# One decoder layer on one core: all five engines get another order of the same steps

## The reference

```python
x = x + attn(layernorm(x))        # attn(z) = z + out-projection; 16 heads of 8, softmax over 128 keys, biases
x = x + xattn(layernorm(x), ctx)  # 16 heads of 64, rope on q and k, key j seen by query i if i-32 <= j <= i
x = x + ffn(layernorm(x))
# ffn: e = argmax(x @ router.T) of 8 experts, for each token
#      y  = (silu(x @ gate[e].T) * (x @ up[e].T)) @ down[e].T      its own expert, hidden size 256
#      ys = the same with one shared expert;  result y + ys
```

## Time and profile before

| | |
|---|---|
| runs | 796.94, 797.93, 798.8 us; median 797.93 |
| profiled execution | 793.82 us, its span 791.7 us |
| TensorE | 755.8 us busy (95%), 11,796 MATMUL |
| TensorE weight loads | 610.1 us (77%) |
| VectorE, ScalarE, GpSimd | 541.6, 535.6, 526.1 us (68%, 68%, 66%) |
| mean granted clock of TensorE | 0.988 |

### The profile page before, as it was taken

One profiled execution on the slowest core, in us unless ns is written; L12 is line 12 of the kernel. 1 busy time (PEld: TensorE's weight loads), 2 busy tenths in 40 slices (PEclk: granted clock), 3 DMA queues, 4 the chain that ended last, 5 costly groups with the idle time before them and its releaser, 6 DMA issues.

```text
span 791.7 us, 31542 instructions
## 1 busy us (share of the span) xinstructions
PE 755.8 (95%) x11796; PEld 610.1 (77%) x11796; DVE 541.6 (68%) x1398; ACT 535.6 (68%) x1943; POOL 526.1 (66%) x857
## 2 busy tenths in 40 slices
PE   7999999999999999999999999999999999788995
PEld 5778888888888888888888888888888887666563
DVE  3467777777777777777777777777777778445663
ACT  2367777777777777777777777777777776664452
POOL 4466677666777677777767766677676776454454
PEclk8999999999999999999999999999999999999997
DMA  6000111001111000000000000000000000343340
GB/s 235 9 9 9 29 37 36 21 29 36 37 36 37 15 14 24 23 23 17 23 24 23 23 15 15 17 15 17 17 13 13 10 10 2 88 161 110 100 116 20
DMA packets 24563, 29.86 MB, mean 38 GB/s; under 512 B 3416, under 2 KB 20700, under 8 KB 24416
## 3 DMA queue, kind: packets, MB, share of 16 engines
q1 hardware_dynamic: 20912, 19.66, 8.2%
q0 software_dynamic: 2784, 6.56, 2.4%
q10 hardware_dynamic: 720, 1.63, 0.6%
HBM read 16.82 MB, written 11.47 MB: 36 GB/s over the span
## 4 chain that ended last, share of the span: by engine, by line
PE 91%; ACT 2%; issue 2%; DVE 2%; another core or an unknown queue 1%; DMA 1%; POOL 1%; POOLq 0%; SPq 0%; ACTq 0%; DVEq 0%
PE P L315 10%; PE P L280 8%; PE P L290 8%; PE P L356 7%; PE P L300 7%; PE P L342 5%; PE P L328 5%; PE P L232 4%; PE P L215 4%; PE P L247 4%; PE P L374 4%; PE P L421 4%; PE P L382 2%; PE P L255 2%; PE P L345 1%
## 5 line engine op out<-in xcount | busy, mean ns | idle before, releaser
L884 ACT ACTIVATE PX<-P,mx 128x128 f32<-128x128 f32 x512 | 182.4, 384 | 25.6 <-DVE mx L596 25.6
L596 DVE TENSOR_REDUCE mx<-P 128x4 f32<-128x512 f32 x128 | 81.2, 679 | 112.9 <-PE P L315 112.9
L1054 POOL TENSOR_TENSOR PX<-PX,mx 128x512 f32<-128x512 f32 x128 | 130.5, 1041 | 40.4 <-DVE mx L601 40.4
L884 ACT ACTIVATION_READ_ACCUMULATOR PX<-P,mx 128x1 f32 x512 | 114.6, 224 | 0.0
L893 ACT ACTIVATE PT<-P 128x512 f32<-128x512 f32 x128 | 69.9, 598 | 65.6 <-PE P L328 65.6
L848 ACT ACTIVATE PS<-P 128x512 f32<-128x512 f32 x128 | 66.1, 602 | 53.5 <-PE P L236 53.5
L1000 POOL TENSOR_SCALAR st<-st 128x1 f32<-128x1 f32 x96 | 22.1, 230 | 120.5 <-DVE st L504 116.8
L1049 POOL TENSOR_TENSOR rq<-rq,tq 128x1024 f32<-128x1024 f32 x32 | 75.6, 2364 | 24.8 <-DVE rq L560 24.8
L315 PE MATMUL P<-rk,rq 32*128 32x128 f32 x2048 | 85.1, 283 | 6.0 <-issue 5.7
L535 DVE TENSOR_REDUCE nmf<-P 128x4 f32<-128x512 f32 x128 | 79.5, 683 | 13.0 <-PE P L215 13.0
L315 PEld LDWEIGHTS P<-rk,rq 32*128 32x128 f32 x2048 | 71.4, 186 | 15.5 <-issue 14.8
(11 more groups left out here) (155 smaller groups left out, 1836.7 us busy)
## 6 DMA issues: line engine op xcount, KB each, us to landing
xrow<-z_xs SPq DMA_DIRECT2D x39, 136.0 KB
ew<-in_ew SPq DMA_DIRECT2D x9, 384.0 KB, 3.3
z_xs<-c SPq DMA_DIRECT2D x8, 408.0 KB
x<-in_x SPq DMA_DIRECT2D x32, 64.0 KB, 1.7
cxT<-in_ctxT SPq DMA_DIRECT2D x31, 64.0 KB, 1.7
z_xs<-c SPq DMA_DIRECT2D x8, 136.0 KB, 1.9
out<-yst,xrow POOLq DMA_INDIRECT x39
wk<-in_wk SPq DMA_DIRECT2D x1, 512.0 KB, 4.1
```

Of the source, the lines that this page charges most:

```text
L596: dve.tensor_reduce(mx[b % 3][:, 0, r, :], v3(bank(f"ds{r}")), AX.X, ALU.max, negate=True).then_inc(S["v_dm"][r], 1)
L884: t = act.activation(PX[(4 * b + r) % 6][:, c, :], p[:, c * 128:c * 128 + 128], ACT.Exp, bias=m[:, 0, r, c:c + 1], scale=1.0, accum_out=m[ ...
L1054: pool.tensor_tensor(X[:, :, :], X[:, :, :], mx[b % 3][:, 2, r, :].rearrange("p (h a) -> p h a", a=1).to_broadcast([128, 4, 128]), ALU.mul ...
```

## The change

No step's own code changes. What changes: the order of the steps in the loop body of all five engines, the banks of the steps (`BANK`), the filling products at the start (`WARM`, 182 before, 241 after), the number of periods (46 to 45), how many expert tiles lie in the loop (`LOOP`), and the order of the first loads. A helper `first` is added that nothing calls; without it `batch` does as before.

```diff
-LOOP = dict(xt=11, xg=10, xr=8, xy=8, xl=21)
+LOOP = dict(xt=13, xg=12, xr=10, xy=9, xl=21)
-WARM = {('a', 0): 36, ('a', 1): 14, ('nmt', 0): 43, ('kE', 1): 13, ('cnt', 0): 13, ('qO', 0): 9, ('ds0', 0): 22,
-        ('cnt', 1): 19, ('nmt', 2): 13}
-S0, PERIODS = 28, 46
+WARM = {('a', 0): 36, ('qkv', 0): 8, ('v1', 0): 17, ('s0', 0): 51, ('nmt', 0): 40, ('st0', 0): 9, ('oT', 0): 13,
+        ('ln', 0): 10, ('qO', 0): 8, ('ds0', 0): 10, ('oT', 1): 28, ('ln', 1): 11}
+S0, PERIODS = 28, 45
```

Going round it the form changes 11 times. GpSimd:

```diff
             for s in range(PERIODS):
-                batch(e_rstd, s - 6)
-                batch(b_rstd, s - 4)
                 batch(d_pn, s - 5, 3)
-                batch(d_pn, s - 5, 2)
+                tile(x_send, "xy", s - 36, 0)
+                batch(f_pos, s - 7)
+                batch(b_nm, s - 3)
...
+                batch(f_send, s - 7)
                 batch(r_ka, s - 3)
-                batch(b_nm, s - 3)
-                batch(f_pos, s - 7)
                 batch(r_qa, s - 4)
-                batch(f_send, s - 7)
+                batch(a_xab, s - 2)
...
                 batch(a_rstd, s)
                 batch(f_acc, s - 6)
-                batch(a_xab, s - 2)
+                batch(d_pn, s - 4, 0)
+                batch(e_rstd, s - 5)
                 batch(d_pn, s - 4, 1)
-                batch(d_pn, s - 4, 0)
+                batch(d_pn, s - 4, 2)
+                batch(b_rstd, s - 3)
```

More of the change, by code:

```diff
@@ L455, in _ @@
[L455 to L461, removed]
-                batch(d_s, s - 5)
+                tile(x_hT, "xr", s - 37, 2)
+                batch(b_x1, s - 5)
+                tile(x_up, "xg", s - 36, 0)
+                batch(b_s, s - 4)
+                tile(x_dn, "xy", s - 37, 2)
@@ new lines, in _ @@
+                batch(e_tr, s - 7)
+                tile(x_hT, "xr", s - 37, 3)
+                tile(x_tr, "xt", s - 36, 2)
+                batch(r_k, s - 4, 1)
+                batch(a_tr, s - 3)
+                tile(x_up, "xg", s - 36, 1)
+                batch(f_up, s - 7)
+                batch(b_ln, s - 5)
+                batch(d_t, s - 6, 0)
+                batch(d_t, s - 6, 1)
+                batch(r_q, s - 5, 1)
+                batch(b_nm, s - 4)
+                batch(r_q, s - 5, 0)
@@ new lines, in _ @@
+                tile(x_dn, "xy", s - 37, 3)
+                batch(d_pv, s - 6, 1)
+                batch(b_st, s - 4)
+                batch(d_pv, s - 6, 0)
+                batch(a_qkv, s - 3)
+                tile(x_hT, "xr", s - 36, 0)
+                tile(x_tr, "xt", s - 36, 3)
+                batch(c_v, s - 4, 0)
+                tile(x_up, "xg", s - 36, 2)
+                batch(d_s, s - 5)
+                tile(x_tr, "xt", s - 35, 0)
+                batch(b_pv, s - 4)
+                batch(d_wo, s - 6)
@@ L463, in _ @@
+                tile(x_dn, "xy", s - 36, 0)
+                tile(x_hT, "xr", s - 36, 1)
+                tile(x_up, "xg", s - 36, 3)
+                batch(f_pos, s - 7)
+                batch(b_oT, s - 4)
                 batch(r_k, s - 3, 0)
[L464 to L467, removed]
                 batch(f_dn, s - 7)
-                batch(a_qkv, s - 3)
-                batch(b_oT, s - 4)
@@ L471, in _ @@
-                batch(d_wo, s - 6)
+                tile(x_dn, "xy", s - 36, 1)
                 batch(b_cn, s - 4)
-                tile(x_up, "xg", s - 36, 1)
-                tile(x_dn, "xy", s - 37, 3)
-                batch(f_pos, s - 7)
[L476 to L482, removed]
@@ L751, in _ @@
             for s in range(PERIODS):
-                tile(x_gate, "xg", s - 37, 1)
-                batch(r_k3, s - 4)
-                tile(x_gate, "xg", s - 37, 2)
+                batch(d_max, s - 6, 1)
+                batch(d_max, s - 6, 3)
+                batch(d_ri, s - 6, 0)
+                batch(d_y, s - 7)
+                tile(x_y, "xy", s - 37, 0)
+                batch(b_cn, s - 5)
+                tile(x_gate, "xg", s - 37, 2)
+                batch(f_pos, s - 8)
+                batch(d_ri, s - 6, 1)
@@ L970, in _ @@
[L970 to L982, removed]
@@ L983, in _ @@
-                batch(b_oT, s - 4)
+                batch(f_th, s - 8)
+                batch(b_cT, s - 6)
+                batch(d_pt, s - 7, 0)
+                batch(d_pt, s - 7, 2)
+                batch(a_norm, s - 3)
+                batch(d_pt, s - 7, 3)
+                batch(d_pt, s - 7, 1)
+                batch(b_nmT, s - 5)
+                batch(d_ox, s - 7, 1)
+                batch(b_ps, s - 5, 1)
+                batch(d_ox, s - 7, 0)
+                tile(x_hT, "xr", s - 37, 0)
@@ new lines, in _ @@
+                tile(x_xT, "xt", s - 37, 3)
+                batch(b_ps, s - 5, 3)
+                batch(b_ps, s - 5, 2)
+                batch(b_ps, s - 5, 0)
+                batch(c_v, s - 5, 0)
+                tile(x_xT, "xt", s - 36, 0)
+                batch(a_q, s - 4)
+                tile(x_th, "xg", s - 37, 2)
+                batch(d_exp, s - 6, 0)
+                batch(b_oT, s - 5)
+                batch(d_exp, s - 6, 1)
+                tile(x_hT, "xr", s - 37, 1)
+                batch(d_exp, s - 6, 2)
```

129 lines of the change are left out of this document (53 added, 76 removed).

## The result

The kernel after takes 767.24 us (median of 4 runs, 765.12 to 768.98), the kernel before 797.43 beside it (4 runs, 796.87 to 798.8): ratio 0.9618, 95% interval 0.9589 to 0.9647. The forecast was 767. The profiled execution took 765.12 us, its span 763.0. Seven lines were added near the top of the file, so line 315 (`d_s`) is now 322, 261 (`b_cn`) is 268, 300 (`r_q`) is 307.

The account below looks back on a forecast made before the run. TensorE's own work bounds the kernel, so its start-to-start period sets the time. Span 791.7 - 24.6 + 2.8 - 6.2 - 1 - 2 = 760.7, plus 6.2 to the median gives 767 us; range 756 to 779.

Parts of the forecast that it names:

- the three middle terms: Middle periods: send moved -24.6 us, +2.8 for what may reach `d_pv`, two fewer tiling changes -6.2.
- Send: GpSimd's send moved from `d_s` to beside `r_q`: saves 0.91 us in each of 27 periods, -24.6 us.
- The +0.1 a period for `d_pv`: Allowance for the moved send's disturbance reaching the small products of `d_pv`: +2.8 us in all.
- Tilings: TensorE's tiling changes, 13 to 11 a period: 0.20 us a period, -6.2 us over 31 periods.
- Slacks: Waits between engines in the new order: all hidden by TensorE's work, costed at nothing; tightest slack 0.1 at `b_oT`.
- The GpSimd chain to `d_s`: Send, `r_ka`, then `r_qa`, which lets `d_s` start: done 11.1 us after `b_s`, slack 0.6.
- The slower rival: GpSimd chain to `d_s`: send and rotation adds 1.9 us longer, `d_s` waits 1.3 every period, 807 us; chance 0.07.
- Ends: Start, earlier loads against 59 more filling products: -1 us (-4 to +3); tail, earlier expert tiles: -2 (-6 to +3).
- From span to median: Added to the 760.7 us span: 2.1 around the span and 4.1 from execution to median, 6.2 in all.
- The stall goes with the send: Rival at the moved send: the 0.91 us a period is paid whatever runs beside it, 789 us; chance 0.10.
- new short waits: Rival at `b_oT` and `b_x1`: slack of 0.1 to 0.2 missing by 0.4 us a period, 779 us; chance 0.12.
- the order moves nothing: Rival: TensorE's work is the same and the pause only shifts to another step, same time; chance 0.03.

## Why the prediction was right

The time and the period were right, and the send's stall is shown; the split of the gain between the two parts was not. Spans of the two first traces, by `b_cn`: the forecast was -31.0, the trace has -28.7: -29.7 from the first to the 31st, where the three middle terms add up to -28.0, and +1.0 outside it, where the ends were forecast at -3.

- **Send** (forecast -24.6 + 2.8). The mechanism held in this: the pause was the send's, and large products cover it. Its fixed rate of 23 instructions a us didn't (77 beside a send in the new order), so why large products cover it stays open. The send came 5.57 after `b_s` (396.24 - 390.67; forecast 5.3). Its worth is 21.16 - 20.19 = 0.97 a period, by the clean period of the kernel with the send moved alone, where I had 0.91; the early `d_s` of the earlier trace rows that I measured from has a small gap of its own. The +0.1 a period for `d_pv` didn't come: both halves of `r_q` keep their times, and `d_pv` behind them too (398.29 - 397.48 = 0.81, and 0.81 for its other half, with no send near).
- **But moving the send alone brings only 18.6 of it** from the first to the 31st `b_cn`: 629.6 before, 611.0 with the send moved, 599.9 after. The step that the forecast lacked is the 7.4 us of late gaps that appear in the long row `b_st`, masks, `d_s`. The new order of TensorE has no such row and almost none of these gaps (1.2 us); whether it is the row or where the instruction packets fall that removed them stays open. So the order brings 11.1 us here, about half of it not by fewer tilings.
- **And the new order alone takes most of the stall away.** I gave the order only its tilings, -6.2. With the send left at `d_s` it brings 22.3 us from the first to the 31st `b_cn` (629.6 before, 607.3; the traces are of two chips), since the stall is 0.31 there and not the 0.91 that I took for a fixed price. In that order the move adds 6.9 more. The sum came out by luck as far as this goes: I credited the send's whole price to its move, and the order gives whatever the move can't collect.
- **Tilings** (forecast 0.20 a period, -6.2). 20.19 against 20.02 is 0.17, and undoing two changes costs 0.29: 0.09 to 0.15 for a change, inside the bounds. (The Trainium skill, TensorEngine Tiling (Array Packing), section Key Properties, has every change of mode drain TensorE. The runs agree: the new neighbours, 64\*64 beside 32\*128 and 32\*128 beside 128\*32, cost no visible extra.)
- **Slacks** (forecast: nothing late). No wait of TensorE on ScalarE or GpSimd stands in its middle, neither at `b_oT` with 0.1 nor at `b_x1`. The GpSimd chain to `d_s` came out at 402.0 - 390.67 = 11.3 after `b_s`, where I had 11.1, and left 0.4 of the 0.6. What it lost is the idle time ahead of the send, 0.46 against the 0.29 of the earlier trace rows. The profile puts 26 of these 32 waits down to VectorE's multiply `tk`, but the code has no semaphore from `tk` to the send, only to `r_ka` behind it, and two sends show that `tk` isn't the cause (GpSimd's and VectorE's timelines):

```profile
195.98 1.11 POOL L1089 DMA_INDIRECT z_xs<-er,pos  x1 [0.46 <-POOL er L1082]
```

```profile
194.99 1.23 DVE L567 TENSOR_TENSOR tk<-P,tab 128x1024 f32<-128x1024 f32 x1 [0.26 <-issue]
```

The multiply runs until 196.22, the send starts at 195.98, and the idle time is 0.46 all the same. (The Trainium skill, SBUF — State Buffer, section Who interferes with whom, says that a VectorE instruction with at most one SBUF input, outside the 2-port modes, doesn't contend with GpSimd. `tk` has one input in PSUM, and the trace agrees: the send beside it takes 1.11, as ever.) What the 0.17 is stays open. The slower rival had a longer chain in mind, ten times as much.
- **Ends** (forecast -1 and -2; measured +0.6 and +0.4 outside the 30 periods). The start was the one term of the wrong sign: the load of `x` of batch 2 did come earlier (VectorE's statistics of it at 11.18 instead of 12.54), but the 51 filling products stand on the path for 2.9 us. In the tail, the interval between the last two `b_cn` grew from 21.4 to 24.0, as more expert tiles are in the loop, and only 2.2 came back behind it. A stop near 680, in which VectorE and ScalarE idle too (3.89 and 2.42 us) while GpSimd goes on sending, cost TensorE 2.8; its cause is open. The products that follow run at a granted clock of 0.5, the 1.2 GHz level, until 686.9 (TensorE's timeline):

```profile
680.43 0.39 PE L445 MATMUL P<-ew,xhT 128*128 x2
683.62 0.42 PE L349 MATMUL P<-PT,V 64*64 64x96 f32 x2 [2.80 <-issue]
```

- **From span to median.** The span was missed by 2.3, and the median lay 2.1 above the profiled execution instead of 4.1. So the time was hit within 0.3 partly by these two cancelling.
- **Rivals.** "The stall goes with the send" is refuted by `r_q`; "new short waits" and "slower chain" by the 536.73 of 537.00; "the order moves nothing" by the time. None of them, and not the forecast, saw that the stall is absent on one chip: there before is at 769.65 and kernels close to the one after at 761.25 to 770.51. By these neighbours the whole change is worth about 1% or less there (an estimate).

## What to carry to other kernels

Look for another engine's instruction that starts at a fixed distance ahead of a pause that the trace can't explain, and move it to where TensorE issues slowly, beside large products. Price the move in the order that will stand afterwards: a long unbroken row of small products has other pauses to offer once the first is gone, and an order without such a row has less of both, so try the order by itself too, and check the banks of what is put in between. Time a kernel on more than one chip before its stalls are taken for the kernel's own, and try a kernel without the filling products that stand between a step and inputs that are already there: here the step came earlier without them on all three chips, though on one the clock fell.

## What the runs showed of the hardware

- An indirect DMA issued by GpSimd slows TensorE's issue on some chips and not on others: in one and the same program, with the send 0.35 ahead, `d_s` took 1.94 us on one chip and 2.24 on another. The kernel before differs by 3.4% between chips (769.65 and 795.6), but a kernel without a send at `d_s` differs too (770.2 and 779.13), mostly behind the last batch. What makes the chips differ stays open, and so does what the send takes from TensorE.
- The pause is tied to the send's start and not to a product: in both traces of the kernel before, at 25 of the first 27 sends, the longest gap in `d_s` is 0.48 to 0.51 us and ends 1.26 to 1.30 us after the send's start, whether 13 products of `d_s` stand ahead of it or 22.
- Its price depends on what TensorE does and did just before: 0.97 us behind a row of small products, 0.31 behind large ones (0.77 to 0.88 and 0.47 where the send starts with `d_s`), 0 beside large ones.
- Without any send, a row of `b_st`, masks and `d_s` (3.4 us of small products) has gaps of 0.15 to 1.2 us in ten of 32 periods in one trace, all of them where an instruction packet of 16 KB starts 0.7 to 1.7 us ahead; in a second trace of the program, eleven gaps of up to 1.56, only six of them in that window. (The Trainium skill, Runtime: NRT & Kernel Launch, section Instruction fetch mechanics, has the fetch hidden behind the rate of issue. If these gaps are fetches, it isn't so in this row.)
- At the start, 1.82 us of idle time ahead of `c_v` was followed by a clock of 0.52, 1.45 was not, and 1.90 with filling products behind `c_v` was not either. The fall cost 0.95 us on `b_s` alone.
